# Query and key projections as three fp32r products of split rows and weights, with Pool reordering the keys, in a relative-position attention and MLP kernel

## What is computed

```python
x = L0_attn_x                                  # (16, 512, 128)
xn = _layernorm(x)
# attention part, on xn normalized once more, with gain and bias
q, k, v = (z @ W + b, split into 16 heads of 8, for Wq, Wk, Wv)
p = (pe @ Wp)                                  # positions, same for all sequences
content = einsum('bihd,bjhd->bhij', q + u_bias, k)
pos = _relative_shift(einsum('bihd,jhd->bhij', q + v_bias, p))
head = softmax((content + pos) * 8 ** -0.5) @ v
attn = head @ Wo + bo
# MLP part
h = relu(s0 * [xn, -xn] @ (+-1)) * 2 ; h = relu(s1 * h @ (+-1)) * 2 ; mlp = s2 * h @ (+-1)
out = x + attn + mlp
```

## Time and profile before

| what | value |
|---|---|
| median of three runs | 1462.28 us |
| the profiled execution | 1461.93 us, of which the span of the program is 1460.0 us |
| granted TensorE clock, mean over the span | 0.994 |
| busy: PE, DVE, ACT, Pool | 1446.1, 1331.8, 1225.3, 724.2 us |
| DRAM traffic over the span | 375 GB/s |

### The profile page before, as it was taken

How to read it: one execution, slowest core, us unless ns; L and a number is a source line. 1 busy time by engine, 2 the same in 40 slices (tenths; PEclk the granted TensorE clock), 3 DMA queues, 4 the chain that set the end, 5 groups by cost and what they waited for, 6 DMA issues and landing times.

```text
span 1460.0 us, 41422 instructions
## 1 busy us (share of the span) xinstructions
PE 1446.1 (99%) x16101; PEld 961.4 (66%) x16101; DVE 1331.8 (91%) x3490; ACT 1225.3 (84%) x1364; POOL 724.2 (50%) x721
## 2 busy tenths in 40 slices
PE   8999999999999999999999999999999999999998
PEld 4566666666666666766666666666666666666666
DVE  5799899998999999899998999999899998989996
ACT  4698888888888888888888888888888888888873
POOL 4556455554555556455554555456455554533410
PEclk9899999999999999999999999999999999999999
DMA  4999999999999999999999999999999999999992
GB/s 148 398 394 396 377 399 391 389 394 377 406 381 389 399 381 400 382 389 391 390 399 373 403 386 391 395 377 397 390 392 394 386 395 383 397 381 380 397 396 97
DMA packets 80723, 550.41 MB, mean 377 GB/s; under 512 B 9360, under 2 KB 10384, under 8 KB 14992
## 3 DMA queue, kind: packets, MB, share of 16 engines
q1 hardware_dynamic: 43376, 278.61, 49.4%
q10 hardware_dynamic: 37152, 269.15, 47.7%
HBM read 274.57 MB, written 273.15 MB: 375 GB/s over the span
## 4 chain that ended last, share of the span: by engine, by line
PE 96%; ACT 1%; DMA 1%; DVE 1%; issue 0%; ACTq 0%
PE ps_pt L795 36%; PE ps_av L809 19%; PE ps_pos L771 15%; PE ps_job L697 12%; PE ps_job L661 4%; PE ps_job L656 4%; PE ps_job L676 2%; ACT pt_sb L470 1%; PE ps_job L672 1%; PE ps_job L684 1%; PE ps_job L667 1%; DMA shift<-pos_sb 1%; PE ps_con L783 1%; DMA c_sb<-in_consts 1%; PE ps_job L678 0%; PE ps_job L680 0%
## 5 line engine op out<-in xcount | busy, mean ns | idle before, releaser
L622 DVE CUSTOM_DVE_ANT_0 sc_sb<-ps_con,sc_sb 128x512 f32<-128x512 f32 x1024 | 662.6, 683 | 91.1 <-PE ps_con L783 86.2
L460 ACT COPY pos_sb<-ps_pos 128x1024 f32<-128x1024 f32 x510 | 518.1, 1016 | 188.4 <-PE ps_pos L771 186.8
L630 DVE TENSOR_SCALAR sc_sb<-sc_sb,nmax 128x512 f32<-128x512 f32 x1024 | 600.7, 618 | 0.1
L795 PE MATMUL ps_pt<-c_sb,sc_sb 128*128 128x128 f32 x4048 | 553.8, 280 | 2.0 <-ACT pt_sb L470 1.1
L470 ACT ACTIVATE pt_sb<-ps_pt 128x1024 f32<-128x1024 f32 x506 | 519.0, 1026 | 13.6 <-PE ps_pt L795 13.5
L795 PEld LDWEIGHTS ps_pt<-c_sb,sc_sb 128*128 128x128 f32 x4048 | 434.2, 141 | 126.6 <-issue 97.1
L809 PE MATMUL ps_av<-pt_sb,v_sb 128*9 128x128 f32 x8192 | 319.9, 274 | 0.6 <-ACT pt_sb L470 0.6
L809 PEld LDWEIGHTS ps_av<-pt_sb,v_sb 128*9 128x9 f32 x8192 | 173.0, 90 | 208.1 <-issue 205.3
L364 POOL CAST h<-act_sb 128x512 fp32r<-128x512 f32 x128 | 81.5, 637 | 393.7 <-ACT act_sb L436 393.5
L783 PE MATMUL ps_con<-k_stack,q_stack 26*128 26x512 f32 x1024 | 261.2, 498 | 0.9 <-DVE nmax L622 0.8
L771 PE MATMUL ps_pos<-p_stack,q_stack 26*128 26x512 f32 x1024 | 260.2, 499 | 1.1 <-ACT pos_sb L460 0.8
(11 more groups left out here) (107 smaller groups left out, 978.1 us busy)
## 6 DMA issues: line engine op xcount, KB each, us to landing
shift<-pos_sb SPq DMA_DIRECT2D x256, 1026.0 KB, 9.3
sc_sb<-shift ACTq DMA_DIRECT2D x256, 1024.0 KB, 9.9
x_sb<-in_x SPq DMA_DIRECT2D x16, 256.0 KB, 11.8
out<-x_sb SPq DMA_DIRECT2D x15, 256.0 KB, 10.5
stack_w_sb<-in_stack_w SPq DMA_DIRECT2D x2, 256.0 KB, 8.2
c_sb<-in_consts ACTq DMA_DIRECT2D x1, 422.0 KB, 7.5
o_t<-in_wp SPq DMA_DIRECT2D x1, 256.0 KB, 3.0
heads<-in_pe_t ACTq DMA_DIRECT2D x1, 256.0 KB, 8.4
```

Of the source, the lines that this page charges most:

```text
L460: act.copy(to, ps_pos[:, :, :]).then_inc(s_pe, 1)
L622: dve.tensor_tensor_reduce(sc_sb[:, m % N_SC, t, :], ps_con[:, k, :], sc_sb[:, m % N_SC, t, :], -SCALE, 3.4e38, ALU.add, ALU.min, nmax[:, ...
L630: dve.tensor_scalar(sc_sb[:, m % N_SC, t, :], sc_sb[:, m % N_SC, t, :], nmax[:, m % N_SC, t:t + 1], None, ALU.subtract).then_inc(s_sub, 1)
L795: last = pe.transpose(pt_banks(k)[:, j % 2, t * P:(t + 1) * P], sc_sb[:, u % N_SC, t, j * P:(j + 1) * P], id_sb)
```

## The change

1. **Products.** For batches 1 to 15 each projection is three fp32r products, high weights by high rows, high weights by low rows, low weights by high rows, added in PSUM (new lines in `job_parts`). That is 15 times 8 projections. Batch 0 is as before.
2. **Rows.** ScalarE writes the scaled TZ to an `act_sb` buffer, and Pool splits it into `z_hl` (a new "TZ" case of `split`). ScalarE's reordering copy to `z_t` stays, since the values still use it.
3. **Keys.** The rows of `z_hl` are in the plain order, so Pool reads the key projection in the other order when it splits it. Its source then steps by 128 elements from one to the next, in both instructions.
4. **Weights.** Pool splits `wq` and `wk` once, at half 13 of the first batch.
5. **Buffers.** `wq`, `wk`, `wp_sb` and the first `z_q` now lie in the last score buffer, a part of the constants in the one before it, and `o_t` in `z_sb`. Three waits come with that: before the first load of the last score buffer, before Pool writes `z_sb` (on the WO job of three batches before), and before the first `z_t` copy. The load of the constants is cut in two DMAs.

```diff
-        c_sb = sb("c_sb", [P, consts.shape[1]])
+        KEPT = consts.shape[1] - 2 * (GROUPS * DH + D)
+        c_sb = sb("c_sb", [P, KEPT])
...
-        stack_w_sb = sb("stack_w_sb", [P, 2, GROUPS * P])
-        wq, wk = stack_w_sb[:, 0, :], stack_w_sb[:, 1, :]
+        wq_hl = sb("wq_hl", [P, 2, GROUPS * P], F32R)
+        wk_hl = sb("wk_hl", [P, 2, GROUPS * P], F32R)
...
-        z_q = sb("z_q", [P, S])
+        z_hl = sb("z_hl", [P, 2, S], F32R)
...
-        o_t = sb("o_t", [P, S])
-        wp_sb, pe_sb = o_t, heads[:, :, :, :].rearrange("p t h d -> p (t h d)")
+        o_t = z_sb[:, :, :].rearrange("p t c -> p (t c)")
+        pe_sb = heads[:, :, :, :].rearrange("p t h d -> p (t h d)")
+
+        wq, wk, wp_sb, z_q = (sc_sb[:, N_SC - 1, k, :] for k in range(4))
+        first_c = sc_sb[:, N_SC - 2, 0, 0:consts.shape[1] - KEPT]
...
-        SPLITS = ("T1", "L0", "L1", "QG", "KG")
+        SPLITS = ("T1", "TZ", "L0", "L1", "QG", "KG")
...
                 wait(pool, s_job, job(("T1", "TZ")[k], b - 1))
+                if k == 1 and b >= 3:
+                    pool.wait_ge(s_job, job("WO", b - 3))
...
-                    dst = dst[:, c, :]
+                    dst, low = dst[:, c, :], low.broadcast_to([P, S])
+                    if name == "KG" and b > 0:
+                        src = src.rearrange("d (t q a) -> d a q t", a=4, t=NT)
+                        dst, low = (v.rearrange("d (a q t) -> d a q t", a=4, t=NT) for v in (dst, low))
...
-                    own(pool.tensor_tensor(dst, src, low.broadcast_to([P, S]), ALU.mult))
+                    own(pool.tensor_tensor(dst, src, low, ALU.mult))
                     pool.tensor_tensor(dst, src, dst.bitcast(F32), ALU.subtract).then_inc(s_hl, 1)
...
+                                 "TZ": (z_hl[:, :, :], max(job("QG", b - 1, GROUPS - 1), job("KG", b - 1, GROUPS - 1))),
...
+                if h == 13:
+                    for hl, raw in ((wq_hl, wq), (wk_hl, wk)):
+                        own(pool.tensor_copy(hl[:, 0, :], raw))
+                        pool.tensor_tensor(hl[:, 1, :], raw, hl[:, 0, :].bitcast(F32), ALU.subtract).then_inc(s_whl, 1)
...
-            act.dma_start(c_sb[:, :], consts).then_inc(s_c, 16)
+            act.dma_start(c_sb[:, :], consts[:, 0:KEPT]).then_inc(s_c, 16)
+            act.dma_start(first_c, consts[:, KEPT:]).then_inc(s_c2, 16)
...
-                    last = act.activation(z_q[:, :], ps_job[:, :], ACT.Identity, bias=BB, scale=G)
+                    last = act.activation(dst, ps_job[:, :], ACT.Identity, bias=BB, scale=G)
...
+                    if u == N_SC - 1:
+                        act.wait_ge(s_whl, 2)
+                        act.wait_ge(s_job, max(job(n, 0, GROUPS - 1) for n in ("PG", "QG", "KG")))
...
+                if name in ("QG", "KG") and b > 0:
+                    if c == 0:
+                        pe.wait_ge(s_hl, ACTS[("TZ", b, 0)] + 1)
+                    hl, cut = (wq_hl, wk_hl)[name == "KG"], slice(c * P, (c + 1) * P)
+                    return [lambda i=i: pe.matmul(out, hl[:, i // 2, cut], z_hl[:, i % 2, :], start=(i == 0), stop=(i == 2))
+                            for i in range(3)]
```

More of the change, by code:

```diff
@@ L67, in attention_mlp @@
         bias_q = const(GROUPS)
[L68 to L72, removed]
-        stack_w_sb = sb("stack_w_sb", [P, 2, GROUPS * P])
-        wq, wk = stack_w_sb[:, 0, :], stack_w_sb[:, 1, :]
+        assert at[0] == KEPT
+        wq_hl = sb("wq_hl", [P, 2, GROUPS * P], F32R)
+        wk_hl = sb("wk_hl", [P, 2, GROUPS * P], F32R)
         bias_k = sb("bias_k", [P, GROUPS])
@@ L108, in attention_mlp @@
         heads = sb("heads", [P, NT, H, DH])
-        o_t = sb("o_t", [P, S])
-        wp_sb, pe_sb = o_t, heads[:, :, :, :].rearrange("p t h d -> p (t h d)")
+        o_t = z_sb[:, :, :].rearrange("p t c -> p (t c)")
+        pe_sb = heads[:, :, :, :].rearrange("p t h d -> p (t h d)")
+        wq, wk, wp_sb, z_q = (sc_sb[:, N_SC - 1, k, :] for k in range(4))
+        first_c = sc_sb[:, N_SC - 2, 0, 0:consts.shape[1] - KEPT]
+        bk_rows, uk_rows = (first_c[:, k * GROUPS * DH:(k + 1) * GROUPS * DH].rearrange("p (g d) -> p g d", d=DH)
+                            for k in range(2))
+        u_all, v_all = (first_c[:, 2 * GROUPS * DH + k * D:2 * GROUPS * DH + (k + 1) * D]
+                        .rearrange("p (h d) -> p h d", d=DH) for k in range(2))
         stage = pt_sb[:, :, :].rearrange("p a c -> p (a c)").bitcast(U8)
@@ L125, in attention_mlp @@
         ps_job = psum("ps_job", [P, S])
-        s_c = sem("s_c")
+        s_c, s_c2 = sem("s_c"), sem("s_c2")
         s_wq, s_wk = sem("s_wq"), sem("s_wk")
@@ L141, in attention_mlp @@
         s_zt = sem("s_zt")
+        s_whl = sem("s_whl")
         s_x1, s_z = sem("s_x1n"), sem("s_z")
@@ L476, in _ @@
                         act.wait_ge(s_jev, ev("TZ", b))
+                        raw = act_sb[:, ACTS[("TZ", b, 0)] % N_ACT, :]
+                        if b == 1:
+                            act.wait_ge(s_job, job("KG", 0, GROUPS - 1))
                         act.copy(z_t[:, :].rearrange("d (a q t) -> d t q a", a=4, t=NT),
-                                 z_q[:, :].rearrange("d (t q a) -> d t q a", a=4, t=NT)).then_inc(s_zt, 1)
+                                 raw.rearrange("d (t q a) -> d t q a", a=4, t=NT)).then_inc(s_zt, 1)
         @block.vector
@@ L565, in heads_first @@
                 return w.rearrange("p (h r) -> p h r", r=32)
+            dve.wait_ge(s_c2, 16)
             for i, (w, by, landed, n) in enumerate(((wp_sb[:, :], v_all, s_wp, 32), (wk, u_all, s_wk, 16))):
```

## The result

The changed kernel takes 1474.34 us (median of 4 runs, 1473.64 to 1475.56), the kernel before in the same session 1462.63: a ratio of 1.0082, 95% interval 1.0069 to 1.0095. It is 11.7 us slower. The forecast was a gain, to 1457. The time lies in the range only because that reached into the second rival.

The account below looks back on a forecast made before the run. PE, busy 99% of the span, was taken to bound the kernel, with DVE setting the pace from half 31 to 5. (-0.16 - 0.25 + 0.05) x 15 = -5.4 us gave a forecast of 1457 us, range 1447 to 1482.

Parts of the forecast that it names:

- the second rival: Halves 0 to 3: Pool holds DVE longer than PE saves, deciding above about e = 0.4; middle 1472 us, chance 0.37.
- The projection's 0.16: Each projection on PE: three fp32r products take 0.70 us instead of 0.86, saving 0.16; 19.2 us at most.
- The price e: Pool's key splits: extra time of each instruction for reading with a step of 128 elements, taken as 0.25 us.
- ScalarE's 0.56: Upper bound for Pool's strided key reads: what ScalarE pays for the same permutation, 0.56 us an instruction.
- The exclusion of Pool and DVE: A DVE subtraction and a two-input Pool instruction exclude each other; whoever is later waits.
- con(2): Start of half 2's content products: later of half 1's start plus 2.71 and DVE's half-1 minima plus 1.41, so 981.06.
- The step that failed: Halves 31 to 5: query split and its hold come 0.3 sooner, starting at 981.06 + 3.24; stretch gives 0.25.
- con(5): Start of half 5's content products: 989.45 against 989.70 before.
- The other projections: Half 27 keeps its 0.16 whole; at halves 9, 10, 14 and 15 longer holds eat up the 4 x 0.16.
- TZ: Halves 23 and 24: fifteen more splits on Pool, covered for PE but holding DVE, taken as 0.05 us a batch.
- The start: Batch 0: weight split, cut constants DMA and three new waits cost nothing, within 1 us either way.
- Rival one: DVE is never late and the strided read costs nothing: all 19.2 us come through, 1443 us; chance 0.07.

Follow-up runs that it names:

- after_again: The changed kernel itself, run again unedited as a control on another chip: 1471.97 us, ratio 1.0075 to the kernel before.
- gate_q1: Changed kernel with Pool's high and low parts of query 1's split each waiting for DVE's subtractions of a given half: 1465.64 us, ratio 1.0028.
- after_gate: Changed kernel with waits placing Pool's query and key split parts behind DVE's subtraction pairs, and two jobs (L0's product 3, key 2) exchanged: 1443.62 us, ratio 0.9888.
- tz_cut: Changed kernel with Pool splitting only 4 of TZ's 512 columns from batch 2 on: 1470.15 us, ratio 1.0055.
- plain_tz_cut: Changed kernel with Pool reading keys in plain order and splitting only 4 of TZ's 512 columns from batch 2 on: 1484.32 us, ratio 1.0146.
- plain_keys: Changed kernel with Pool reading the keys in plain order, without the reordering: 1485.51 us, ratio 1.0152.
- the other table: Kernel before with another table of jobs, moving keys, queries, L0's products and others to different halves: 1469.71 us, ratio 1.0064.

## Why the prediction was wrong

*Right.* The projection's 0.16: halves with one are 2.71 long. The price e: 0.28 for the high part and 0.25 for the low one, where I took 0.25. ScalarE's 0.56 was far too high, and so was the estimate of 0.43 that I had worked out from the cycles in the Trainium skill (GPSIMD Engine Reference, Performance pitfalls for Q7 kernels): for these two-input instructions the measurement decides. ("More than twice as long as ScalarE" held for Pool's 1.28 alone; 1.04 is 1.8 times 0.58.) The exclusion of Pool and DVE, and halves 0 to 3 as its place, were right too. con(2) came 2.71 after con(1), and the second key split 3.24 after con(1), as computed. That 3.24 was part luck: what released the split is given as half 2's content product, which ended at 988.79, and not ScalarE's eviction, which ended at 988.75.

*The step that failed* is in the stretch from half 31 to 5: "The query split and its hold come out 0.3 sooner, since it starts at 981.06 + 3.24." That is 984.30, but by the line before it the key's low part ends at 984.50, so Pool cannot start the query then. It goes on 0.24 behind the low part, while the held first subtraction still runs, and that is the worst order that I had named myself from the earlier trace rows. The trace shows just this, 0.24 and a pair of 2.62.

The order hangs on hundredths of a microsecond. A held subtraction ends 0.28 after its release (979.04 against 978.76, 993.42 against 993.14 above), so 0.24 is just where the first one ends, and the query part can go either way. It went between the two in 11 of batches 1 to 15 here and in 4 of them in the control (after_again). In the others it went in behind the second. Its low part then held the first subtraction of half 3, and the cast behind it came between the two, as before the change. The control's halves 2 and 3 at the same place, DVE and then Pool:

```profile
990.71 1.75 DVE L653 TENSOR_SCALAR sc_sb<-sc_sb,nmax 128x512 f32<-128x512 f32 x2
...
993.60 2.23 DVE L653 TENSOR_SCALAR sc_sb<-sc_sb,nmax 128x512 f32<-128x512 f32 x2
```

```profile
992.02 1.34 POOL L365 TENSOR_TENSOR q_stack<-act_sb,c_sb 128x512 fp32r<-128x512 f32 x1 [0.24 <-POOL k_stack L366]
993.43 1.27 POOL L366 TENSOR_TENSOR q_stack<-act_sb,q_stack 128x512 fp32r<-128x512 f32 x1
994.94 0.61 POOL L375 CAST h<-act_sb 128x512 fp32r<-128x512 f32 x1 [0.23 <-POOL q_stack L366]
```

Halves 31 to 5 take 20.2 us in batches of the first kind and 19.7 in those of the second, against 19.53 before. So the two kinds differ by 0.5, and both lose. In the second kind con(5) comes within 0.1 of what I computed, and the loss falls in half 5 (3.30 against 2.94), one half beyond where my working stopped. Holding back the query alone (gate_q1) ends both kinds.

What moved was Pool's cover: before, the query waited 0.31 for ScalarE; now it waits for Pool itself, in 31 places of the span:

```profile
POOL q_stack L365 <- POOL k_stack L366: 7.6, 31, 0.5
```

Instead of 0.25 gained, the stretch from half 31 to the end of half 4 lost 0.56 a batch (16.59 to 17.15, means over the batches); to the end of half 5 it lost 0.62, and 0.31 in the control.

*The other projections.* I let the holds at 14 and 15 eat up PE's 0.32 and no more. Halves 14 to 18 lost 0.53 (with the waits of after_gate they take 14.02, against 14.08 before). Halves 9 to 13 came out as counted, at +0.01, and half 27 gave its 0.17. The batch, measured as the sum of its halves, lost 0.97.

*TZ.* I took 0.05 a batch. tz_cut's ratio says about 0.26 and plain_tz_cut's 0.06, both with intervals that reach nothing, so this term is neither confirmed nor refuted.

*The start.* I counted nothing. The changed kernel is 1.8 us ahead at the first mark above, which is half 0 of batch 2. It gets ahead before the first new product runs. In the kernel before, PE's first transposes wait for the constants; in the changed one, with that load cut in two, they start 1.25 us sooner (before, then after):

```profile
9.57 0.66 PE L684 MATMUL ps_pt<-c_sb,z_sb 128*128 128x128 f32 x4 [1.69 <-DMA c_sb<-in_consts]
```

```profile
8.32 0.60 PE L713 MATMUL ps_pt<-c_sb,z_sb 128*128 128x128 f32 x4
```

The first content product is 2.80 sooner (39.53 against 42.33). In between, from 30 to 34 us, the windows show PE at a granted clock of 0.53 and 0.62 before, near the lower of its two levels (1.2 GHz), and of 1.00 after; in the 2 us ahead of that, PE had been busy 0.49 before. The columns are window, its length, busy time and records of PE, PEld, DVE, ACT and Pool, granted clock, DMA share, GB/s:

```profile
28.00:30.00 2.00, 0.49 (x4) 0.34 (x3) 1.56 (x3) 1.01 (x1) 1.74 (x2) 1.00 0.79 332
30.00:32.00 2.00, 2.00 (x7) 0.81 (x5) 0.00 (x0) 0.69 (x1) 1.73 (x3) 0.53 0.47 193
32.00:34.00 2.00, 2.00 (x5) 0.98 (x4) 0.00 (x0) 1.13 (x2) 1.42 (x2) 0.62 0.00 0
```

```profile
30.00:32.00 2.00, 2.00 (x6) 0.94 (x6) 0.09 (x1) 1.68 (x2) 1.75 (x3) 1.00 0.03 8
32.00:34.00 2.00, 2.00 (x10) 0.98 (x8) 1.97 (x3) 1.19 (x2) 1.92 (x3) 1.00 0.99 345
```

No run tested how much of the lead is the load's and how much the clock's. It is no fixed sum either: the control has 2.65 of it at the first content product and 0.6 at the first mark.

*The rivals.* Rival two came true, but not by its threshold: I let it decide above e = 0.4, and it decided at 0.25 to 0.28. Its mechanism, Pool between the two subtractions, is the one that the trace shows. Its deciding quantity was not e. plain_keys has e = 0 and is the slower, after_gate has e whole and is the faster. Rival one's time, 1443, was within reach of the change, but only in the order of after_gate. I had only asked how long Pool's instructions are, and gave the order one sentence among the doubts.

*What stays open.* Which of the two kinds a batch takes, why gate_q1's profile is longer in halves 9 to 18, why the other table costs the kernel before 0.6%, and how much of the loss in halves 14 to 18 is the key's low part and how much the cast; no run held one without the other.

## What to carry to other kernels

Where two engines exclude each other, write the starts and ends of both beside each other, and check after each computed time which of them is asked for when the other ends; a start that is computed from one releaser must be the latest of all, its own engine's last instruction among them. An engine with half its time idle can set the pace of a full one, and a wait that places its work behind the other's pair can be worth more than shorter work. Such a wait also holds what is queued behind it, so look there before adding it.

## What the runs showed of the hardware

- Two subtractions in a row on VectorE, each 0.47 us by itself, are no unit: a Pool instruction asked for during the first went ahead of the second, and in the rows shown the pair took 1.95 to 2.73 us instead of 0.87. The Trainium skill (SBUF — State Buffer, Who interferes with whom) says that when VectorE runs in a mode that takes both port pairs, which it lists for `tensor_scalar`, whichever issues first gets the shared pair for its whole instruction and the other blocks; the holds here agree (the pair of 990.80 ends 0.28 after Pool's 993.14).
- Pool's strided reads cost 0.25 to 0.28 us for 512 elements in a two-input instruction of 1.28 or 1.04 us.
- Asked for 0.24 us behind the instruction that had held the first subtraction, Pool's next went ahead of the second in 11 of 15 batches in one execution and in 4 of 15 in another of the same kernel.
- Reordering alone cost 24 us, the products with plain keys 23, both together 12, with intervals of some 2 us either way: shifts of some tenths of a microsecond turned the order over.
